# x as a plain load into the rows of x1 and a TensorE addition, in place of an adding DMA

## What is computed

```python
h = _layernorm(x) * (1 + ca) + sa
x = x + ga * attn(h)        # attn(h) = h + y @ W_out, y from a state-space scan
h = _layernorm(x) * (1 + cb) + sb
x = x + gb * ffn(h)         # 16 experts of which each token uses 4
```

## Time and profile before

| | us |
|---|---|
| median of 3 runs | 2814.53 |
| lowest, highest | 2812.36, 2818.06 |
| the profiled execution | 2817.6 |
| its span, first to last instruction | 2815.9 |

### The profile page before, as it was taken

How to read it: one execution, slowest core, us unless ns; L and a number is a source line. 1 busy time by engine, 2 the same in 40 slices (tenths; PEclk the granted TensorE clock), 3 DMA queues, 4 the chain that set the end, 5 groups by cost and what they waited for, 6 DMA issues and landing times.

```text
span 2815.9 us, 29019 instructions
## 1 busy us (share of the span) xinstructions
PE 2370.4 (84%) x9004; PEld 1660.7 (59%) x9004; DVE 2429.2 (86%) x2450; ACT 1565.5 (56%) x2961; POOL 2237.4 (79%) x1563
## 2 busy tenths in 40 slices
PE   3445799989979898898989899898989989898899
PEld 1222466566656666675666667565666656566678
DVE  2678898989999898999999899998989899899932
ACT  3555665655566556655665665566565556665311
POOL 1578878888888888888888888888888888887922
PEclk8676898999999899999999999999999999999999
DMA  4689798898989899898999989898998989898921
GB/s 112 174 201 230 198 240 219 219 240 202 238 215 234 218 227 240 212 240 209 238 222 233 234 209 235 216 237 215 236 229 209 237 203 239 208 242 214 238 68 49
DMA packets 338380, 596.80 MB, mean 212 GB/s; under 512 B 49696, under 2 KB 160288, under 8 KB 338224
## 3 DMA queue, kind: packets, MB, share of 16 engines
q0 software_dynamic: 72960, 243.30, 45.5%
q1 hardware_dynamic: 265264, 351.64, 39.5%
HBM read 349.89 MB, written 10.06 MB: 128 GB/s over the span
## 4 chain that ended last, share of the span: by engine, by line
PE 40%; DVE 25%; issue 12%; POOL 8%; ACT 8%; DMA 6%; SPq 1%; DVEq 0%; POOLq 0%; ACTq 0%
DVE hbank L726 14%; PE wbank L498 14%; PE mbank L510 6%; PE wbank L440 4%; PE wbank L526 4%; PE wbank L400 4%; POOL unit L1199 3%; PE wbank L388 3%; PE wbank L523 2%; DMA gsum<-unit 2%; DVE unit L740 2%; DVE act L704 2%; DMA w_scratch<-rows_out 2%; ACT z L849 2%; DMA w_all<-w_scratch 2%
## 5 line engine op out<-in xcount | busy, mean ns | idle before, releaser
L1199 POOL TENSOR_TENSOR unit<-dtx,b_bc 128x1024 f32<-128x1024 f32 x512 | 1358.7, 2662 | 9.0 <-DMA b_bc<-bc_scratch 6.8
L726 DVE TENSOR_TENSOR_SCAN hbank<-hbank,unit 128x1024 f32<-128x1024 f32 x512 | 1173.4, 2292 | 100.6 <-ACT hbank L1028 92.0
L1028 ACT ACTIVATE hbank<-dt,a_neg 128x512 f32<-128x512 f32 x1024 | 668.9, 681 | 325.3 <-DVE unit L740 291.2
L1211 POOL DMA_DIRECT2D gsum<-unit x448 | 451.1, 1007 | 152.8 <-DMA gsum<-unit 72.8
L740 DVE TENSOR_TENSOR unit<-hbank,c_bc 128x1024 f32<-128x1024 f32 x448 | 545.7, 1218 | 20.9 <-DMA c_bc<-bc_scratch 1.4
L510 PE MATMUL mbank<-down_t,act 128*128 128x256 f32 x2048 | 513.7, 389 | 58.9 <-POOL act L1166 36.1
L1166 POOL TENSOR_TENSOR act<-act,w_all 128x512 f32<-128x512 f32 x256 | 360.4, 1408 | 249.9 <-DVE act L704 231.1
L498 PE MATMUL wbank<-h_t,gate_t 128*128 128x256 f32 x2048 | 498.5, 387 | 25.6 <-DVE act L704 14.2
L498 PE MATMUL wbank<-h_t,up_t 128*128 128x256 f32 x2048 | 486.9, 380 | 15.4 <-DVE gz L608 13.6
L510 PEld LDWEIGHTS mbank<-down_t,act 128*128 128x128 f32 x2048 | 388.6, 193 | 159.3 <-issue 61.9
L498 PEld LDWEIGHTS wbank<-h_t,gate_t 128*128 128x128 f32 x2048 | 388.0, 192 | 129.7 <-DVE act L704 28.4
(11 more groups left out here) (121 smaller groups left out, 2382.9 us busy)
## 6 DMA issues: line engine op xcount, KB each, us to landing
gsum<-unit POOLq DMA_DIRECT2D x448, 512.0 KB, 7.4
c_bc<-bc_scratch SPq DMA_DIRECT2D x464, 256.0 KB, 5.5
b_bc<-bc_scratch SPq DMA_DIRECT2D x448, 256.0 KB, 6.2
w_all<-w_scratch SPq DMA_DIRECT2D x256, 256.0 KB, 4.5
ht<-in_L_attn_x_dram SPq DMA_DIRECT2D x16, 512.0 KB, 8.5
w_out<-in_L_attn_W_out_dram SPq DMA_DIRECT2D x16, 512.0 KB, 10.2
ht<-in_L_attn_x_dram POOLq DMA_DIRECT2D x16, 512.0 KB, 10.3
out_dram<-xt SPq DMA_DIRECT2D x16, 512.0 KB, 3.4
```

Source lines behind the costliest of these rows:

```text
L726: eng.tensor_tensor_scan(h, h, unit[:, g % RING, :, :].rearrange("p a t -> p (a t)"), 0.0, ALU.mult, ALU.add).then_inc(scanned, 1)
L1028: eng.activation(hbank[g % HB][:, a, :], dt[:, 2 * q + a, :], ACT.Exp, scale=a_neg[:, 2 * q + a, n:n + 1]).then_inc(decayed, 1)
L1199: eng.tensor_tensor(unit[:, g % RING, :, :], dtx[:, 2 * q:2 * q + 2, :], b_bc[:, s:s + 1, :].to_broadcast([P, 2, T]), ALU.mult).then_inc(d ...
L1211: eng.dma_start(gsum[:, (2 * p + k) % SUMS, :, :], unit[:, g % RING, :, :], accum_op=ALU.add).then_inc(summed[k], 16)
```

## The change

x is loaded by SP (`load_res`, moments 66 to 70 of the slot) into the rows of `xt` that are to hold x1. It waits for the output of two rows before to be written, in the first two rows for the last staged weight chunk to be turned. `scale_h` has one step (moment 58) and issues no DMA. PE's `project` waits for `h_scaled` as well and adds two identity matmuls for each token tile, one with `ht` and one with `xt`.

```diff
-                     ("scale_h", slot, 2, 56, 58), ("gates", slot, 9, 36, 42),
+                     ("scale_h", slot, 1, 56, 58), ("load_res", slot, 1, 66, 70), ("gates", slot, 9, 36, 42),
...
                     need.wait_ge(wo_made, row + 1)
+                    need.wait_ge(h_scaled, row + 1)
                     need.wait_ge(res_in, 16 * (row + 1))
...
-                        m = eng.matmul(t.bank[:, u * H:(u + 1) * H], ident[:, :], ht[:, row % 2, h * TT // 2 + u, :],
-                                       start=False, stop=True)
+                        for res in (ht, xt):
+                            m = eng.matmul(t.bank[:, u * H:(u + 1) * H], ident[:, :],
+                                           res[:, row % 2, h * TT // 2 + u, :], start=False, stop=res is xt)
...
                 eng.tensor_tensor(h, h, ga_row[:, :].rearrange("p (a h) -> p a h", a=1).to_broadcast([P, TT, H]),
                                   ALU.mult).then_inc(h_scaled, 1)
                 yield
-                need.wait_ge(h_scaled, row + 1)
-                eng.dma_start(h, d["L0_attn_x"][row].rearrange("(t p) h -> p t h", p=P), accum_op=ALU.add).then_inc(
-                    res_in, 16)
-                yield
...
+            def load_res(row):
+                if row >= 2:
+                    need.wait_ge(row_out, 16 * (row - 1))
+                else:
+                    t = work.at["turned", len(chunks) - 1, 1]
+                    need.wait_ge(t.full, t.after)
+                eng.dma_start(xt[:, row % 2, :, :], d["L0_attn_x"][row].rearrange("(t p) h -> p t h", p=P)).then_inc(
+                    res_in, 16)
+                yield
```

More of the change, by code:

```diff
@@ L1397, in _ @@
             need.wait_ge(mod_out, 16)
-            stage_of = {"load_x": load_x, "load_wo": load_wo, "load_ga": load_ga, "load_gb": load_gb, "rows_bc": rows_bc,
+            stage_of = {"load_x": load_x, "load_wo": load_wo, "load_res": load_res, "load_ga": load_ga, "load_gb": load_gb, "rows_bc": rows_bc,
                         "weigh": weigh, "chunks": lambda r: turning}
```

## The result

| | before | changed |
|---|---|---|
| median, us | 2814.2 | 2840.4 |
| lowest to highest | 2812.4 to 2818.1 | 2838.2 to 2842.0 |
| the profiled execution's span | 2815.9 | 2838.8 |

The two medians lie 26.2 us apart. The ratio estimated from all runs is 1.0085 (95% interval 1.0073 to 1.0097), which is 24 us slower, between 21 and 27. The forecast was 27.3 us.

What follows compares the result with a forecast made beforehand. In most rows PE leads, ACT passes delay to DVE and POOL; in the last, POOL and accumulating DMAs bound. 27.9 - 1.2 - 1.1 + 1.7 = +27.3 us gave median 2841.8 us, own range 2834 to 2849.

Steps and rivals of the forecast that it cites:

- Count and price of a twin: PE's projection: 64 second identity matmuls reading xt, two records and 0.43 us each, 27.9 us in all.
- The rule of one pass per column: PE's extra matmuls: 262 cycles for 256 columns, an estimated 7 us for 64, sum near +6 us; put aside.
- The way it takes: Behind the projection: PE delays ACT's xt copies by 0.86 and 1.72 us; ACT's decays, then DVE's scans, wait longer.
- I charge it whole: PE's extra matmuls: nothing runs free past ACT's copies, so all 27.9 us count.
- slots last 1.7 us longer each, except the last: Sign in the slot times: each 1.7 us longer, the last about 1 us less than that.
- The moves: POOL's work and x's load between queues: -1.2 and -1.1 us in row 15, +1.7 in row 0.
- this buys nothing in the middle rows: POOL gets back 0.8 to 1.4 us per row, but later idles 2.48 us for DVE: 0 gained there.
- Rival B: POOL and the accumulate paced every row; each of 16 gets 2.3 us back: -9 us, median 2806, chance 0.08.
- -2.3 us: Row 15: -1.2 us for the x issue leaving POOL, -1.1 us for the load changing DMA queues.
- rival C: SP's queue: the x load makes c rows land late, 1.0 us in each of 16 rows, median 2858, chance 0.09.
- +1.7 us: Row 0: the new load comes just ahead of the chain's gsum DMA; taken from between -1.1 and +1.7 us.
- The wait on h_scaled: PE ahead of the projection: scale_h ends some 80 us before it is needed, so zero cost.

Runs made afterwards that it cites:

- the later copies: ACT's copies out of the projection's bank two moments later: on the changed kernel, ratio 1.0080 to the kernel before; on the kernel before, ratio 0.9986.
- the twins alone: Kernel before with the projection's identity matmul issued twice through half the identity, nothing moved: ratio 1.0077, +22 us (18 to 25).
- the load at 56: Changed kernel with the plain load of x at moments 56 to 58 instead of 66 to 70: ratio 1.0088 to the kernel before.
- the third matmul: Changed kernel with ht added by two matmuls through half the identity, one more matmul per token tile: ratio 1.0176, +50 us on the kernel before.
- move alone: Changed kernel without the projection's identity matmul of ht, so as many matmuls as before: ratio 0.9992 to the kernel before, -2 us (-5 to 0).

## Why the prediction was right, and where it was off

**Count and price of a twin: right.** 64 matmuls, 128 records, 0.43 us each pair. In the pieces of the chain above, four records hold PE for 0.86 us. The rule of one pass per column was rightly put aside. Of the four times, the Trainium skill has the reason on another page ("FP8 and Floating Point Precision", section "TensorE Precision Notes"): a true fp32 product takes four passes. The trace agrees in size: 0.43 us for 256 columns at a granted clock of 1.00.

**The way it takes: right.** Units 6 and 8 grew by 0.86 us each, in all slots 2 to 14. The prediction named the decays behind the copies and the normalisation that starts from them. What it did not name, and what the later copies show, is the experts' tanh and the experts' matmuls behind the twins in PE's own queue: with the decays out of the way, these hand on the whole 1.73 us.

**The sum: 27.3 forecast, 24 measured (21 to 27).** The forecast is at the edge of the interval. The first twin alone gave 22 us (18 to 25), the further one on top of it 28, where PE's own work is 27.9. So the step that is over-sized is "I charge it whole", and, as far as the noise lets one tell, only for the first. By place, the changed kernel's profile against the two of the kernel before: units 6 to 8 of slots 2 to 14 +22.5 us (13 slots of 1.73, whole), units 9 to 19 of these slots -2.5 and -7.1, the last slot +3.2 and +2.7, and all else cancels to under half a microsecond. The sign "slots last 1.7 us longer each, except the last" thus came out as 1.5 and 1.2 us on average, and the last slot, for which less was forecast, gained most.

What units 9 to 19 gave back can in part be seen in unit 19. It takes either 7.2 or 8.7 us. The long form stood in 5 of slots 2 to 14 before, in 5 when run again, in 2 in the changed kernel, in 1 with the twins alone. PE's clock explains the two forms. Of the kernel before, the stretch ahead of unit 19 in slots 8 and 9 (columns as in the earlier trace rows):

```profile
1475.40:1478.80 3.40, 3.40 (x12) 2.03 (x11) 3.37 (x3) 1.94 (x4) 3.40 (x3) 1.00 0.83 285
1637.10:1640.50 3.40, 3.40 (x8) 2.14 (x7) 3.37 (x3) 1.80 (x4) 3.40 (x3) 0.51 0.88 298
```

and PE in slot 8, then in slot 9, then DVE in slot 9:

```profile
1474.59 1.99 PE L498 MATMUL wbank<-h_t,gate_t 128*128 128x256 f32 x8 [1.07 <-DVE act L704]
1476.42 1.02 PE L523 MATMUL wbank<-xb,diag_d 128*128 128x512 f32 x2
```

```profile
1636.27 2.95 PE L498 MATMUL wbank<-h_t,gate_t 128*128 128x256 f32 x8 [1.07 <-DVE act L704]
1639.01 1.80 PE L523 MATMUL wbank<-xb,diag_d 128*128 128x512 f32 x2
```

```profile
1646.82 0.75 DVE L580 SCALAR_TENSOR_TENSOR z<-wbank,conv_w,z 128x511 f32<-128x511 f32 x1 [1.84 <-ACT z L901]
```

The granted clock is 1.00 in one and 0.51, the lower level of 1.2 GHz, in the other; the same matmuls take 1.7 us longer, and DVE then waits 1.84 us where it waited 0.57 in slot 8. This holds in all 13 profiles: from 2.5 us ahead of unit 19 to 0.9 behind its start the granted clock is 0.50 to 0.63 at every form of 8.6 or 8.7 us, and 1.00 at every other. Unit 10 goes the same way: from 2 us ahead to 5 behind the clock is 0.95 to 1.00 where it takes 5.4 us, and 0.65 to 0.76 where it takes 6.2 to 7.5.

Three long forms fewer, at 1.44 us between long and short, are 4.3 us. Against the first profile, though, unit 10 takes as much back (from 5.74 to 6.08 us in each of 13 slots, 4.4 us); against the second it is level. And unit 19 does not show that the twins make these stretches rarer: the five profiles with twins have 2, 1, 2, 0 and 1 long forms, the eight without have 5, 5, 1, 3, 1, 1, 4 and 1. The mean granted clock of the whole run, which is on record for nearly every run, says more. In the 17 runs with one twin (the changed kernel, the twins alone, ACT's copies later, the load at 56) it is 0.938 to 0.942. In the 61 runs of the kernel before beside the experiments it is 0.927 to 0.939, on average 0.933, and among them a run was 0.6 to 1.2 us shorter for each 0.001 more; so 0.007 more is worth an estimated 4 to 8 us. With x added on POOL and no twin it is 0.933 to 0.938. With the third matmul it is only 0.931 to 0.938, and there the further twin cost its full 28 us. So a clock that was at its lower level less often fits what the first twin gave back. Why one twin has this effect and two have not stays open, and so does whether it holds for the pair of the result, where the one clock on record of the kernel before is 0.939. In the Trainium skill, "TensorE: Matmul & The Clock Gate", section "What's actually happening", the clock is said to follow how busy the array was. The last two idle times of PE ahead of the stretch are the same in both slots (0.76 and 1.07 us). One further ahead is not: nine microseconds before unit 19, PE waited 0.88 us for ACT's line 849 in slot 8 and 1.48 in slot 9. In five profiles (the kernel before twice, changed, twins alone, move alone) this wait was 1.31 to 1.59 us ahead of 13 of the 14 long forms, but as long ahead of about a quarter of the 51 short ones, so it goes with the lower clock and does not decide it alone.

**The moves: right in sum, wrong in their parts.** Forecast were -1.2 - 1.1 + 1.7 = -0.6 us; measured -2 (-5 to 0). For POOL and the accumulate "this buys nothing in the middle rows" held, by the run without any load of x. Rival B is out.

In slot 15 I expected -2.3 us. Units 20 to 30 took 49.2 us before, 47.6 without x and 49.8 in the changed kernel. In the other profiles they took 49.3 to 50.0 with the accumulate and 49.5 to 50.0 with the plain load, so either costs about 2 us there, and which costs more cannot be told. The saving was there: against the first profile unit 21 is 0.8 and unit 24 1.1 us shorter, against the second unit 20 1.5 and unit 24 0.6. But unit 26 went from 4.9 to 7.4 us. Here rival C, which I held for unlikely, happened. The issues on SP in slot 15 of the changed kernel, the landing of the b rows issued between 2655 and 2675, the chain, and DVE in unit 26:

```profile
2659.47 0.86 SPq L1283 DMA_DIRECT2D xt<-in_L_attn_x_dram  x1
2660.37 1.94 SPq L1337 DMA_DIRECT2D b_bc<-bc_scratch  x1
2662.35 0.52 SPq L1347 DMA_DIRECT2D c_bc<-bc_scratch  x1
```

```profile
DMA to landing us min/median/max: 6.9/12.6/14.0
```

```profile
2658.88 1.49 POOL unit L1197
2660.37 14.02 DMA b_bc<-bc_scratch
...
2676.76 8.42 DMA gsum<-unit
2685.71 7.79 DMA gsum<-unit
```

```profile
2675.07 1.22 DVE L742 TENSOR_TENSOR unit<-hbank,c_bc 128x1024 f32<-128x1024 f32 x1 [2.56 <-DMA c_bc<-bc_scratch]
```

The b row behind the load took 14.0 us to land and stands in the chain, though POOL waited only 0.53 us for it. The c row issued behind it held DVE for 2.56 us, which is what unit 26 grew by, and the run with the move alone has the same unit at 7.1. So for slot 15 the sum of -1.2 and -1.1 us lacked C's term: a plain load stands in SP's queue ahead of rows with a deadline, and that cost 2.5 us, where C had been priced at 1.0. In the middle slots C did not happen, as forecast. In slot 0, where I took +1.7 us, units 20 to 31 take 53.3 to 54.8 us among the runs in no order that follows the load: not settled, and small.

**The wait on h_scaled** cost nothing: ahead of line 441 PE waits 4.6 us for DVE in the whole run, as before, and for POOL not at all.

## What to carry to other kernels

An instruction on an engine that is busy without a gap, in front of a copy for which an in-order engine waits, costs its full issue time in every repetition, and busy shares don't show it: take it from the chain of waits, count records against instructions of the program, and look for every path that starts behind it before hoping that a reordering hides it. How much of it the clock gives back was a matter of a few microseconds here, and not forecast. Work that a fixed order puts on an engine with spare time is free only in front of that engine's idle time: the same addition on POOL cost 30 us in one place and 8 in another.

## What was not expected

The 16-row pattern repeats to 0.01 us: unit 6 takes 3.77 us in every slot from 2 to 14 before and 4.63 after, while units 10 and 19 switch between a few values (7.2 and 8.7 us for unit 19), each time with PE's granted clock at half for a part of the stretch. And a load of 512 KB that the middle slots never notice, by either queue, costs about 2 us in the last slot alone, where the other work has ended and accumulating DMAs, one behind the other, set the pace; moving the plain load twelve moments forward moved the cost and didn't remove it.
